# Graph network block on one core: packed key one-hots, made by six per-partition compares a window

## The chip, the cores and the metric

The kernel runs on one core of a Trainium2 chip. The metric is the device time of one execution in microseconds (us). TensorE, VectorE, ScalarE, GpSimd and SyncE run their own instruction streams and meet at semaphores.

## The reference

1250 nodes with 768 features and 40000 edges (src, dst), sorted by dst. A layer norm with relu, then a two-layer graph attention network (4 heads of 512, then one of 768), added to x; again a layer norm with relu, then two graph convolutions, added to x. Cut to what matters here:

```
h = relu(layernorm(x))
x = x + gat(elu(gat(h, 4 heads)), 1 head)     # softmax over the edges of each dst
h = relu(layernorm(x))
x = x + gcn(relu(gcn(h)))                     # sums over edges, scaled by degrees
gat: h = x @ W ; e = leaky_relu(al_s[src] + al_d[dst]) ; out[dst] = sum softmax(e) * h[src]
```

## The kernel before

Sparse sums are made dense. A matrix `counts` [src, dst], in ten src tiles of 128 rows, holds how many edges go from src to dst. Later stages use it as a factor of the weights. It is made on TensorE in the stage `first_layer`, beside the first product h = x @ W1.

**Edges.** The 40000 edges lie in 320 chunks of 125 (one edge a partition). The dst range is cut into 80 windows (`NW`) of 16 nodes. Because the edges are sorted, a window needs few chunks: `FIX` = 6 fixed ones each, and what is left goes through `extra_chunks`, a loop with one round here. An edge has a low part (src & 127, 0 to 127) and a key (dst in the window x 10 + src >> 7, 0 to 159, `WK` = 160). For each chunk the one-hot of the low parts (125 x 128) times the one-hot of the keys (125 x 160) adds the edge to its cell.

**One-hots (VectorE).** `count_hot(wd)` (L803) makes both one-hots of all six chunks of a window in one compare (L807): `codes` [125, 2, 160, 6] against `parts_of[:, wd]` [125, 2, 6], spread over the 160 values. The two halves are told apart by an offset of 16384 in codes and parts of the key half. The result goes to one of `SLOTS` = 7 slots of `hot` and lies as [half, value, chunk]: the values of one chunk are 6 bf16 elements, 12 bytes, apart.

**Counts (TensorE).** `count(wd)` (L1141) waits for `hot_ready` and runs six matmuls (L1147), one a chunk, with stationary operand hot[..., 0, 0:128, i] and moving operand hot[..., 1, :, i], both with the step of 12 bytes. The last one frees the slot (`hot_used`). ScalarE copies a group of three windows from PSUM to counts (`count_out`, L694).

**Order around the change.** It is written out by hand. TensorE runs 30 h tiles (`FIRST`; three heads of ten), each 18 f32 matmuls of 512 columns (`tile(n)`, L1134). After each of tiles 0 to 26 come the counts of `windows_after(n)`, 2 or 3 windows; after tile 28 `count_extra` (L1155). VectorE runs, for each n, the one-hots of the same windows, then `columns(n)` (four `attention_column`s, L858, for n = 0 to 2, 10 to 12, 20 to 22 and 26 to 28), `extra_chunks` (L814 to L849) at n = 28, and `weight_lo` (L801) at n = 9, 19 and 29. ScalarE copies each h tile to `stage` (L704), rounds the next head's weights (`weight_hi`, L689), and copies groups of counts. SyncE spills each stage slot (two slots) to memory (L640) and loads the next head's W1 at n = 6, 16 and 22, the last one behind a wait for the columns of head 2. Before this stage, `front` prepares the edges: GpSimd makes `codes` (L289), and VectorE makes parts_of (L421, L422).

Of the kernel before, what the change touches and what calls it, by code (L numbers as in the profile page):

```python
# [5 lines left out]
fp32 = mybir.dt.float32  # L6
f32r = mybir.dt.float32r
bf16 = mybir.dt.bfloat16
u16 = mybir.dt.uint16
i32 = mybir.dt.int32  # L10
ALU = mybir.AluOpType
# [3 lines left out]
P = 128  # L15
# [14 lines left out]
EC = 125  # L30
# [5 lines left out]
NW = NP // WD  # L36
WK = WD * T
FIX = 6
SLOTS = 7
OFFSET = 16384  # L40
# [43 lines left out]
class Memory:  # L84

    def __init__(self, nc, keep):
        base = (nc.sbuf_base + 31) // 32 * 32
# [29 lines left out]
        self.codes = edges("codes", [EC, 2, WK, FIX], u16)  # L117
        self.parts_of = edges("parts_of", [EC, NW, 2, FIX], u16)
# [10 lines left out]
        self.hot = heads("hot", [EC, SLOTS, 2, WK, FIX], bf16)  # L129
# [72 lines left out]
def front(nc, st, mem, x, src, dst, load_weights, tile_in):  # L202
# [3 lines left out]
    codes, parts_of, place, low, key = mem.codes, mem.parts_of, mem.place, mem.low, mem.key  # L206
# [52 lines left out]
    with nc.Block() as block:  # L259
# [9 lines left out]
        def _(pool_):  # L269
# [9 lines left out]
            nc.gpsimd.iota(base[:, :, :], pattern=[[-WK, NW], [0, FIX]], base=OFFSET, channel_multiplier=0).then_inc(made, 1)  # L279
# [9 lines left out]
            nc.gpsimd.iota(codes[:, :, :, :], pattern=[[OFFSET, 2], [1, WK], [0, FIX]], base=0, channel_multiplier=0).then_inc(made, 1)  # L289
# [61 lines left out]
        def _(dve):  # L351
# [61 lines left out]
            def window_parts():  # L413
                n = NW * FIX
                dve.wait_ge(picked, 1)
                chain(nc.vector.tensor_copy(s_i[:, :], p_e[:, 0, 0:n]), False)
                chain(nc.vector.scalar_tensor_tensor(out=d_f[:, :], in0=p_e[:, 1, 0:n], scalar=float(T),
                                                     in1=base_f[:, :, :].rearrange("e w i -> e (w i)"), op0=ALU.mult, op1=ALU.add))
                chain(nc.vector.tensor_scalar(s_hi[:, :], s_i[:, :], 7, None, ALU.logical_shift_right), False)
                chain(nc.vector.tensor_scalar(s_lo[:, :], s_i[:, :], P - 1, None, ALU.bitwise_and))  # L420
                chain(nc.vector.tensor_copy(parts_of[:, :, 0, :], s_lo[:, :].rearrange("e (w i) -> e w i", i=FIX)), False)  # L421
                chain(nc.vector.tensor_tensor(parts_of[:, :, 1, :], d_f[:, :].rearrange("e (w i) -> e w i", i=FIX),  # L422
                                              s_hi[:, :].rearrange("e (w i) -> e w i", i=FIX), ALU.add))
# [100 lines left out]
def first_layer(nc, st, mem, W2, b1, as2, ad2, h_scratch, w_in, a_in, load_weights, tile_in):  # L524
# [3 lines left out]
    xT, codes, parts_of, place, low, key = mem.xT, mem.codes, mem.parts_of, mem.place, mem.low, mem.key  # L528
# [85 lines left out]
    def count_bank(g):  # L614
        return banks[:, 2 + g % 2, :]
# [13 lines left out]
    with nc.Block() as block:  # L629
# [162 lines left out]
        def _(dve):  # L792
# [11 lines left out]
            def count_hot(wd):  # L804
                if wd >= SLOTS:
                    dve.wait_ge(hot_used, wd - SLOTS + 1)
                nc.vector.tensor_tensor(hot[:, wd % SLOTS, :, :, :], codes[:, :, :, :],  # L807
                                        parts_of[:, wd, :, :].unsqueeze(2).to_broadcast([EC, 2, WK, FIX]),
                                        ALU.is_equal).then_inc(hot_ready, 1)
# [308 lines left out]
        def _(pe):  # L1118
# [22 lines left out]
            def count(wd):  # L1141
                g, at = wd // WG, wd % WG * WK
                if at == 0 and g >= 2:
                    pe.wait_ge(win_out, g - 1)
                pe.wait_ge(hot_ready, wd + 1)
                for i in range(FIX):
                    last = nc.tensor.matmul(count_bank(g)[:, at:at + WK], hot[:, wd % SLOTS, 0, 0:P, i], hot[:, wd % SLOTS, 1, :, i],  # L1147
                                            start=i == 0, stop=i == FIX - 1)
                last.then_inc(hot_used, 1)
# [832 lines left out]
```

## Time and profile before

| | |
|---|---|
| median of 3 runs | 1326.92 us (1325.04 to 1327.08) |
| the profiled execution | 1326.07 us |
| its span, first to last instruction | 1324.2 us |
| TensorE (PE) busy | 1227.1 us |
| TensorE weight loads (PEld) | 1107.6 us |
| VectorE (DVE) busy | 850.8 us |
| ScalarE (ACT) busy | 510.6 us |
| mean granted TensorE clock | 0.952 of 2.4 GHz |

The profile is of one execution. Busy time is the union of the instructions' spans on an engine. Matmuls overlap in their rows: the duration of one is longer than the distance from its start to the next start, and it is that distance that TensorE's time is made of. The same holds, less so, for VectorE. In a timeline a row with xN merges N equal instructions, and its second number is the time from the first's start to the last's end.

### The profile page before, as it was taken

To read this page: it belongs to the slowest core of one execution; us is meant where nothing else is said; L and a number is where in the kernel's file an instruction comes from. 1 tells how busy PE (TensorE), PEld (TensorE's weight loads), DVE (VectorE), ACT (ScalarE), POOL (GpSimd) and SP (SyncE) were. 2 spreads that over 40 slices of the span, in tenths; PEclk is the share of its full clock that TensorE was granted. 3 is DMA by queue.
4 is the path that set the end of the run, shared out by engine and by line. 5 is a ranking of instruction groups with operands and counts; after the bars stand their busy time and mean duration, and the time that the engine had idled before them with its cause. 6 is when DMAs were issued, how large, how long until landed. Compare 5 with 4: busy or idle time off the path is not lost. (4 is left out here: it accounts for less than half of the span.)

```text
span 1324.2 us, 17459 instructions
## 1 busy us (share of the span) xinstructions
PE 1227.1 (93%) x7119; PEld 1107.6 (84%) x7119; DVE 850.8 (64%) x1372; ACT 510.6 (39%) x1037; POOL 25.5 (2%) x39
## 2 busy tenths in 40 slices
PE   2799999999989999999999999995899999999998
PEld 2576676776779999999999999994799999989998
DVE  7952733647579768876887678857886652351253
ACT  1311212112165555555555565512544552152111
POOL 5000000000010000000000000000000000000000
PEclk9788888889999999999999999997899999999999
DMA  5003021300011020102010201000310220010131
GB/s 189 14 27 96 31 57 64 91 29 25 0 56 49 1 80 1 49 1 80 1 48 1 80 1 49 1 0 13 117 48 25 92 73 1 1 36 0 65 113 58
DMA packets 27618, 58.44 MB, mean 44 GB/s; under 512 B 3492, under 2 KB 6152, under 8 KB 27536
## 3 DMA queue, kind: packets, MB, share of 16 engines
q1 hardware_dynamic: 27344, 56.96, 13.1%
q8 instruction: 59, 0.97, 0.3%
q10 hardware_dynamic: 192, 0.32, 0.1%
q14 instruction: 23, 0.19, 0.0%
HBM read 41.73 MB, written 15.54 MB: 43 GB/s over the span
## 5 line engine op out<-in xcount | busy, mean ns | idle before, releaser
L1250 PE MATMUL banks<-hs,ring_hi 128*128 128x258 f32 (+1 forms) x1600 | 300.7, 289 | 4.0 <-DVE ring_lo L507 2.1
L1250 PEld LDWEIGHTS banks<-hs,ring_hi 128*128 128x128 f32 (+1 forms) x1600 | 249.0, 189 | 5.7 <-issue 2.5
L1250 PE MATMUL banks<-hs,ring_lo 128*128 128x258 f32 (+1 forms) x800 | 227.4, 284 | 0.0
L481 ACT ACTIVATE e<-banks,al 128x256 f32<-128x256 f32 (+1 forms) x500 | 194.0, 491 | 22.4 <-PE banks L466 22.4
L1250 PEld LDWEIGHTS banks<-hs,ring_lo 128*128 128x128 f32 (+1 forms) x800 | 151.4, 189 | 0.0
L489 ACT ACTIVATE ring_hi<-pf 128x512 fp32r<-128x512 f32 (+1 forms) x125 | 81.7, 654 | 158.6 <-DVE pf L500 155.4
L807 DVE TENSOR_TENSOR hot<-codes,parts_of 125x1920 bf16<-125x1920 uint16 x80 | 90.2, 1155 | 78.9 <-PE banks L1147 78.6
L1278 PE MATMUL banks<-w_hi,oT_hi 128*128 128x384 f32 (+1 forms) x320 | 110.3, 345 | 11.3 <-DVE rows L997 5.5
L1134 PE MATMUL banks<-w_hi,xT_hi 128*128 128x512 f32 x240 | 111.7, 466 | 3.5 <-DVE w_lo L801 3.5
L1147 PE MATMUL banks<-hot 125*128 125x160 bf16 x480 | 110.2, 401 | 0.0
L498 DVE TENSOR_TENSOR e<-e 128x512 f32<-128x512 f32 (+1 forms) x125 | 84.5, 676 | 39.1 <-ACT e L481 39.0
L1278 PE MATMUL banks<-w_lo,oT_hi 128*128 128x384 f32 (+1 forms) x320 | 109.5, 342 | 0.0
L1278 PE MATMUL banks<-w_hi,oT_lo 128*128 128x384 f32 (+1 forms) x320 | 109.5, 342 | 0.0
L1134 PE MATMUL banks<-w_hi,xT_lo 128*128 128x512 f32 x240 | 104.8, 436 | 0.0
L1134 PE MATMUL banks<-w_lo,xT_hi 128*128 128x512 f32 x240 | 104.4, 435 | 0.0
L1147 PEld LDWEIGHTS banks<-hot 125*128 125x128 bf16 x480 | 58.6, 128 | 45.8 <-issue 7.1
L704 ACT ACTIVATE stage<-banks 128x512 f32<-128x512 f32 x30 | 17.9, 595 | 183.3 <-PE banks L1134 183.3
L500 DVE SCALAR_TENSOR_TENSOR pf<-e,counts 128x512 f32<-128x512 f32 (+1 forms) x125 | 85.0, 680 | 4.3
L507 DVE TENSOR_TENSOR ring_lo<-pf,ring_hi 128x512 fp32r<-128x512 f32 (+1 forms) x125 | 84.1, 673 | 2.3 <-ACT ring_hi L489 1.7
L1829 PE MATMUL banks<-hs_hi,ring_hi 128*128 128x386 f32 x200 | 70.4, 352 | 7.8 <-DVE ring_lo L507 6.3
L997 DVE TENSOR_TENSOR rows<-rows,banks 128x384 f32<-128x384 f32 (+1 forms) x80 | 43.9, 551 | 45.5 <-PE banks L1278 44.3
L1278 PEld LDWEIGHTS banks<-w_hi,oT_hi 128*128 128x128 f32 (+1 forms) x320 | 60.3, 189 | 13.7 <-DVE rows L997 6.8
(267 smaller groups left out, 2250.3 us busy)
## 6 DMA issues: line engine op xcount, KB each, us to landing
h_scratch<-stage SPq DMA_DIRECT2D x30, 256.0 KB, 2.0
hs<-h_scratch SPq DMA_DIRECT2D x30, 256.0 KB, 2.9
w_st<-in_L_gnn_W SPq DMA_DIRECT2D x4, 1536.0 KB, 10.2
w_st<-in_L_gnn_W SPq DMA_DIRECT2D x16, 384.0 KB, 3.5
gw_st<-in_L_gnn_W SPq DMA_DIRECT2D x12, 384.0 KB, 3.8
xr<-in_x SPq DMA_DIRECT2D x9, 384.0 KB, 6.8
rows<-in_x SPq DMA_DIRECT2D x9, 384.0 KB, 3.4
x_scratch<-rows SPq DMA_DIRECT2D x9, 384.0 KB
```

Source lines behind the costliest of these rows:

```text
L481: last = nc.scalar.activation(self.e[:, local % 2, a, i, 0:n], self.p_shift[:, a, 0:n], ACT.Exp, bias=scores[a][:, g * G + i:g * G + i + 1])
L489: nc.scalar.activation(self.ring[0][:, g, :, 0:n], self.pf[:, (c * NG + g) % 2, :, 0:n], ACT.Copy)\
L498: nc.vector.tensor_tensor(e[:, 0], e[:, 0], e[:, 1], ALU.max).then_inc(self.e_max, 1)
L500: nc.vector.scalar_tensor_tensor(out=self.pf[:, local % 2, :, 0:n], in0=e[:, 0], scalar=1.0, in1=counts[:, g * G:(g + 1) * G, d0:d0 + n], ...
L507: nc.vector.tensor_tensor(self.ring[1][:, g, :, 0:n], self.pf[:, (c * NG + g) % 2, :, 0:n], self.ring[0][:, g, :, 0:n].bitcast(fp32), ALU. ...
L807: nc.vector.tensor_tensor(hot[:, wd % SLOTS, :, :, :], codes[:, :, :, :], parts_of[:, wd, :, :].unsqueeze(2).to_broadcast([EC, 2, WK, FIX] ...
L997: nc.vector.tensor_tensor(acc, acc, p_g[i % 2][0:m, 0:HALF], ALU.add).then_inc(g_out, 1)
L1134: last = nc.tensor.matmul(p_h[n % 2], xT[a][:, k, t * P:(t + 1) * P], w[b][:, k, :], start=u == 0, stop=u == 3 * KD - 1)
L1147: last = nc.tensor.matmul(count_bank(g)[:, at:at + WK], hot[:, wd % SLOTS, 0, 0:P, i], hot[:, wd % SLOTS, 1, :, i], start=i == 0, stop=i = ...
L1250: last = nc.tensor.matmul(p_a[0:m, dt, half, 0:HH], wt.ring[a][:, s // G, s % G, dt * P:dt * P + m], hs[:, s, b, half * HH:(half + 1) * HH ...
L1278: last = nc.tensor.matmul(p_g[i % 2][0:m, 0:HALF], oT[a][:, k, dt * P:dt * P + m], w2[b][:, k, half * HALF:(half + 1) * HALF], start=j == ...
L1829: last = nc.tensor.matmul(p_a(t)[0:m, half, 0:AH], wt.ring[a][:, s // G, s % G, dt * P:dt * P + m], hs[b][:, s, half * AH:(half + 1) * AH] ...
```

## The change

- `hot` becomes one flat row a slot: first the low one-hots as [value, chunk] (768 elements, step 12 bytes as before), then for each chunk its key one-hot as a packed row of 160.
- `count_hot` makes the low half with one compare of two tensors (768 elements), and each of the six key one-hots with a compare of `place` (0, 1, 2, ... in 16 bits) against a per-partition fp32 key, `keys_of[:, wd, i]`. The slot's semaphore is raised by the last of them.
- The matmuls take the same stationary values at the same step, and a packed moving operand.
- codes has the low half alone; parts_of has the low parts, in 16 bits; keys_of is new, in fp32; the offset of 16384 is gone.

```diff
-        self.codes = edges("codes", [EC, 2, WK, FIX], u16)
-        self.parts_of = edges("parts_of", [EC, NW, 2, FIX], u16)
+        self.codes = edges("codes", [EC, P, FIX], u16)
+        self.parts_of = edges("parts_of", [EC, NW, FIX], u16)
+        self.keys_of = edges("keys_of", [EC, NW, FIX], fp32)
...
-        self.hot = heads("hot", [EC, SLOTS, 2, WK, FIX], bf16)
+        self.hot = heads("hot", [EC, SLOTS, FIX * (P + WK)], bf16)
...
-            nc.gpsimd.iota(base[:, :, :], pattern=[[-WK, NW], [0, FIX]], base=OFFSET, channel_multiplier=0).then_inc(made, 1)
+            nc.gpsimd.iota(base[:, :, :], pattern=[[-WK, NW], [0, FIX]], base=0, channel_multiplier=0).then_inc(made, 1)
...
-            nc.gpsimd.iota(codes[:, :, :, :], pattern=[[OFFSET, 2], [1, WK], [0, FIX]], base=0, channel_multiplier=0).then_inc(made, 1)
+            nc.gpsimd.iota(codes[:, :, :], pattern=[[1, P], [0, FIX]], base=0, channel_multiplier=0).then_inc(made, 1)
...
-                chain(nc.vector.tensor_copy(parts_of[:, :, 0, :], s_lo[:, :].rearrange("e (w i) -> e w i", i=FIX)), False)
-                chain(nc.vector.tensor_tensor(parts_of[:, :, 1, :], d_f[:, :].rearrange("e (w i) -> e w i", i=FIX),
+                chain(nc.vector.tensor_copy(parts_of[:, :, :], s_lo[:, :].rearrange("e (w i) -> e w i", i=FIX)), False)
+                chain(nc.vector.tensor_tensor(keys_of[:, :, :], d_f[:, :].rearrange("e (w i) -> e w i", i=FIX),
                                               s_hi[:, :].rearrange("e (w i) -> e w i", i=FIX), ALU.add))
...
-                nc.vector.tensor_tensor(hot[:, wd % SLOTS, :, :, :], codes[:, :, :, :],
-                                        parts_of[:, wd, :, :].unsqueeze(2).to_broadcast([EC, 2, WK, FIX]),
-                                        ALU.is_equal).then_inc(hot_ready, 1)
+                part = hot[:, wd % SLOTS, :]
+                nc.vector.tensor_tensor(part[:, 0:FIX * P].rearrange("e (v i) -> e v i", i=FIX), codes[:, :, :],
+                                        parts_of[:, wd, :].unsqueeze(1).to_broadcast([EC, P, FIX]), ALU.is_equal)
+                for i in range(FIX):
+                    last = nc.vector.tensor_scalar(part[:, FIX * P + i * WK:FIX * P + (i + 1) * WK], place[0:EC, 0:WK],
+                                                   keys_of[:, wd, i:i + 1], None, ALU.is_equal)
+                last.then_inc(hot_ready, 1)
...
+                part = hot[:, wd % SLOTS, :]
+                lows = part[:, 0:FIX * P].rearrange("e (v i) -> e i v", i=FIX)
                 for i in range(FIX):
-                    last = nc.tensor.matmul(count_bank(g)[:, at:at + WK], hot[:, wd % SLOTS, 0, 0:P, i], hot[:, wd % SLOTS, 1, :, i],
+                    last = nc.tensor.matmul(count_bank(g)[:, at:at + WK], lows[:, i, :], part[:, FIX * P + i * WK:FIX * P + (i + 1) * WK],
```

On TensorE, ScalarE and SyncE the order of instructions is the same. On VectorE each compare becomes seven instructions. The place is VectorE's queue from the columns of tile 0 on, through tile 1's windows to the first column of tile 1 (L858 before, L863 now, is an attention column with the read of its sum). Before:

```order
L858 ISA vcol 128x1
L807 TENSOR_TENSOR hot<-codes,parts_of 125x1920 x3
L858 ISA junk,vcol<-w_st,abc 128x512 [waits v_done]
L858 ISA vcol 128x1
L858 ISA junk,vcol<-w_st,abc 128x512 [waits v_done]
```

Now:

```order
L863 ISA vcol 128x1
L809 TENSOR_TENSOR hot<-codes,parts_of 125x768
L812 TENSOR_SCALAR hot<-place,keys_of 125x160 x6
L809 TENSOR_TENSOR hot<-codes,parts_of 125x768
L812 TENSOR_SCALAR hot<-place,keys_of 125x160 x6
L809 TENSOR_TENSOR hot<-codes,parts_of 125x768
L812 TENSOR_SCALAR hot<-place,keys_of 125x160 x6
L863 ISA junk,vcol<-w_st,abc 128x512 [waits v_done]
```

Three instructions have become 21, in the same place between the columns. From the third window of tile 2 on, the first instruction of a window waits for a free slot. Before:

```order
L807 TENSOR_TENSOR hot<-codes,parts_of 125x1920 x2
L807 TENSOR_TENSOR hot<-codes,parts_of 125x1920 [waits hot_used]
L858 ISA junk,vcol<-w_st,abc 128x512 [waits v_done]
L858 ISA vcol 128x1
```

Now:

```order
L809 TENSOR_TENSOR hot<-codes,parts_of 125x768
L812 TENSOR_SCALAR hot<-place,keys_of 125x160 x6
L809 TENSOR_TENSOR hot<-codes,parts_of 125x768 [waits hot_used]
L812 TENSOR_SCALAR hot<-place,keys_of 125x160 x6
L863 ISA junk,vcol<-w_st,abc 128x512 [waits v_done]
```

The wait stands at the window's first instruction in both.

## Rows read from the trace of the kernel before

**Rows 1.** The page's part 1: engine, busy us (share), instructions.
```profile
PE 1227.1 (93%) x7119; PEld 1107.6 (84%) x7119; DVE 850.8 (64%) x1372; ACT 510.6 (39%) x1037; POOL 25.5 (2%) x39
```

**Rows 2.** The page's part 5: group, count | busy us, mean ns | idle before, releaser.
```profile
L807 DVE TENSOR_TENSOR hot<-codes,parts_of 125x1920 bf16<-125x1920 uint16 x80 | 90.2, 1155 | 78.9 <-PE banks L1147 78.6
...
L1147 PE MATMUL banks<-hot 125*128 125x160 bf16 x480 | 110.2, 401 | 0.0
```

**Rows 3.** Timeline around one count stretch: start us, us, engine, line, operation, count.
```profile
150.09 0.39 PE L1134 MATMUL banks<-w_hi,xT_lo 128*128 128x512 f32 x1
...
153.50 0.39 PE L1134 MATMUL banks<-w_hi,xT_lo 128*128 128x512 f32 x1
...
153.72 4.13 PE L1147 MATMUL banks<-hot 125*128 125x160 bf16 x18
...
157.51 0.77 PE L1134 MATMUL banks<-w_hi,xT_hi 128*128 128x512 f32 x1
...
158.51 0.63 PE L1134 MATMUL banks<-w_hi,xT_lo 128*128 128x512 f32 x1
...
158.94 0.63 PE L1134 MATMUL banks<-w_hi,xT_hi 128*128 128x512 f32 x1
```

**Rows 4.** Windows: stretch, length, busy of PE, PEld, DVE, ACT, POOL, granted clock, DMA.
```profile
57.30:294.00 236.70, 236.70 (x950) 164.99 (x949) 124.05 (x184) 38.31 (x65) 0.00 (x0) 0.88 0.18 57
```

**Rows 5.** By source line, the count matmuls, then the extra chunk's: ns min/median/max.
```profile
L1147 PEld LDWEIGHTS banks<-hot x480: 124/127/145, 57.3 to 293.7; 125*128 125x128 bf16 x160
L1147 PE MATMUL banks<-hot x480: 392/402/403, 57.4 to 293.9; 125*128 125x160 bf16 x160
...
L1155 PEld LDWEIGHTS banks<-extra x1: 96/96/96, 303.8 to 303.8; 125*128 125x128 bf16 x1
L1155 PE MATMUL banks<-extra x1: 243/243/243, 303.8 to 303.8; 125*128 125x160 bf16 x1
```

**Rows 6.** Timeline of TensorE in the attention sums.
```profile
702.80 0.28 PE L1250 MATMUL banks<-hs,ring_lo 128*128 128x258 f32 x1
...
702.93 0.19 PEld L1250 LDWEIGHTS banks<-hs,ring_hi 128*128 128x128 f32 x1
...
703.16 0.28 PE L1250 MATMUL banks<-hs,ring_lo 128*128 128x258 f32 x1
```

**Rows 7.** Timeline of VectorE: one-hot compares, attention columns, the extra chunk's compares.
```profile
70.29 7.57 DVE L807 TENSOR_TENSOR hot<-codes,parts_of 125x1920 bf16<-125x1920 uint16 x7
...
151.97 0.68 DVE L858 CUSTOM_DVE_ANT_0 junk<-w_st,abc 128x512 bf16<-128x512 f32 x1
...
152.58 0.68 DVE L858 CUSTOM_DVE_ANT_0 junk<-w_st,abc 128x512 bf16<-128x512 f32 x1
...
299.69 0.27 DVE L844 TENSOR_SCALAR extra<-place,own_low 125x160 bf16<-125x160 uint16 x1
...
299.87 0.26 DVE L845 TENSOR_SCALAR extra<-place,own_key 125x160 bf16<-125x160 uint16 x1
```

**Rows 8.** Timeline of 20 small matmuls, and windows of the stretches around and behind them.
```profile
324.43 2.39 PE L1178 MATMUL banks<-ident,al_row 8*128 8x8 f32 x20
...
324.40:328.00 3.60, 3.60 (x26) 3.35 (x26) 3.50 (x7) 1.87 (x2) 0.00 (x0) 1.00 0.02 5
328.00:331.50 3.50, 3.50 (x10) 2.70 (x9) 3.43 (x3) 0.00 (x0) 0.00 (x0) 0.51 0.00 0
```

**Rows 9.** Timeline of VectorE, the first instruction of extra_chunks.
```profile
295.75 0.06 DVE L814 MEMSET round__493<- 128x1 f32 x1 [11.96 <-ACT counts L694]
```

**Rows 10.** The page's part 6: DMA issues, KB each, median us to landing.
```profile
h_scratch<-stage SPq DMA_DIRECT2D x30, 256.0 KB, 2.0
...
w_st<-in_L_gnn_W SPq DMA_DIRECT2D x4, 1536.0 KB, 10.2
```

**Rows 11.** Timeline of GpSimd in front.
```profile
3.84 2.81 POOL L289 IOTA codes<- 125x1920 uint16 x1
...
20.27 11.78 POOL L293 TENSOR_SCALAR xr<-xr,rstd,nmr 128x768 f32<-128x768 f32 x10 [13.26 <-DVE nmr L431]
```

More of the change, by code:

```diff
@@ L205, in front @@
     ident, ones, pick, xT = mem.ident, mem.ones, mem.pick, mem.xT
-    codes, parts_of, place, low, key = mem.codes, mem.parts_of, mem.place, mem.low, mem.key
+    codes, parts_of, keys_of, place, low, key = mem.codes, mem.parts_of, mem.keys_of, mem.place, mem.low, mem.key
     until, reach, total = mem.until, mem.reach, mem.total
@@ L527, in first_layer @@
     mask, rows, vcol, deg = mem.mask, mem.rows, mem.vcol, mem.deg
-    xT, codes, parts_of, place, low, key = mem.xT, mem.codes, mem.parts_of, mem.place, mem.low, mem.key
+    xT, codes, parts_of, keys_of, place, low, key = mem.xT, mem.codes, mem.parts_of, mem.keys_of, mem.place, mem.low, mem.key
     until, reach, total = mem.until, mem.reach, mem.total
```

## The prediction

> **What bounds the kernel now.** I read the engine table first. TensorE is busy for 93% of the span and VectorE for 64% [rows 1], so what counts is time on TensorE. The groups by cost then show the two instructions that the change touches [rows 2]. The 480 count matmuls are busy for 110.2 us, and the 80 one-hot compares on VectorE sat idle 78.9 us before they ran, nearly all of it for TensorE. So VectorE is ahead of TensorE in this stage and waits for a free slot of the seven. The place is the stretch from 57 to 294 us, in which h tiles 0 to 26 alternate with the counts of two or three windows each.
>
> The timeline of one tile gives the prices [rows 3]. The f32 matmuls of 512 columns start 0.227 us apart ((153.50 - 150.09) / 15), so a tile of 18 takes 4.09 us. The 18 count matmuls take 157.51 - 153.72 = 3.79 us, 0.2105 us each, though each streams only 160 columns. Right behind them the f32 matmuls start 0.43 us apart (158.51 to 158.94): that is the lower clock, 1.2 GHz. Over the whole stretch the granted clock is 0.88 [rows 4], so 0.12 x 236.7 = 28 us are lost to it. The stretch adds up: 26 x 4.09 + 480 x 0.2105 + 28 = 235 us against 236.7.
>
> **TensorE's part of the change.** The moving operand (key one-hots) goes from a step of 12 bytes to a packed row; the stationary one (low one-hots) keeps its 12-byte step. The kernel holds one packed count matmul of the same shape, the extra chunk's: 243 ns against 402 ns, and its weight load 96 ns against 127 ns [rows 5]. The 159 ns are 160 columns at about 1 ns more each, which fits a moving read that is too slow when strided. A packed operand leaves 160 / 2.4 GHz = 67 ns of streaming. The 512-column matmul takes 227 ns for 213 ns of streaming, 14 ns over, and I add that: 0.081 us each. The weight loads stay strided. The f32 matmuls of 258 columns start (703.16 - 702.80) / 3 = 0.12 us apart beside weight loads of 0.19 us [rows 6], so a load longer than the spacing is covered by the matmul in front; a strided load of 0.127 us should be too. Gain: 480 x (0.2105 - 0.081) = 62 us. Bounds: 0.067 (no gap at all) to 0.127 (loads of 127 ns not overlapped among themselves).
>
> The clock: it falls after 3.79 us in which the array streamed 67 of every 210 ns. Afterwards that stretch is 18 x 0.081 = 1.46 us, 67 of 81 ns streaming. The nearest row is the 20 matmuls of 8 columns, 2.39 us with almost nothing streamed: the clock stood at full through 328 us and then fell to 0.51 for 3.5 us [rows 8]. The new stretch is shorter and dense, so I expect the full clock back, 28 us. The Trainium skill (TensorE: Matmul & The Clock Gate, Part 1) says that the default is throttled and that activity releases it; by it too a denser stretch is kept at 2.4 GHz, and the fall in rows 3 behind sparse counts agrees.
>
> **VectorE's part.** Today one compare of 1920 elements takes (7.57 - 1.16) / 6 = 1.07 us a window. The new one has 768 elements: by proportion 0.43 us, and 0.47 with a fixed share that doesn't shrink. The six key compares have an exact counterpart in the extra chunk's code, a 125x160 compare with an fp32 per-partition key: the two start 0.18 us apart, each lasting 0.26 to 0.27 [rows 7]. Six at 0.18 are 1.08 us. A window costs 0.47 + 1.08 = 1.55 us, 0.48 more than now, 38 us more in 80 windows. Bounds of one key compare: 0.09 (its share of the 1920-element row) to 0.265 (no overlap with the next). The Trainium skill (VectorE: DVE Perf Modes, the errata section) gives 58 cycles and a quarter of the elements for such an operation, 102 ns; by that figure a window would cost VectorE no more than now, and no wait below would arise. The row at 0.18 decides.
>
> Does that cover hold? A tile now costs TensorE 4.09 + 1.46 = 5.55 us, VectorE 3 x 1.55 = 4.65 us. That is still covered. But in tiles 0 to 2, 10 to 12 and 20 to 22 VectorE also makes four attention columns of 0.61 us [rows 7], 2.45 us together: 7.1 us. Neither the first tiles nor those behind a weight_lo (which ties VectorE to TensorE at tiles 9 and 19) have slots in hand, so TensorE waits some 1.55 us in each of nine tiles (shifted by one, tiles 1 to 3, 11 to 13, 21 to 23): 14 us. In these the counts are spread out and the clock may fall as now. Most of such a slow phase lies inside the next wait; for the last tile of each run I keep 1.5 us, 4 us in all. Everything else behind that semaphore moves with it.
>
> The end of the stage: VectorE sat idle 11.96 us before extra_chunks [rows 9], waiting for the last counts. Its work from there (12 columns, 7.3 us, and the chunk, 4.4 us) now starts with the last counts, against two tiles, 8.2 us, on TensorE. With VectorE some 3 us ahead by tile 26 this costs 0.5 us; with no lead 3.5.
>
> Weight and scratch DMAs: W1's load lands 10.2 us after issue, a spill of h 2.0 us [rows 10], and SyncE issues both in order. At tile 22 the load also waits for columns(22), which are now late: it lands some 16 us after that tile, and the spill behind it at about 18.5. ScalarE's copy of tile 24 waits for that spill; TensorE needs that copy for tile 26, at about 21 us. Covered, with 2 us to spare. On GpSimd codes gets shorter (2.81 us now), but the engine idles 13.26 us behind it [rows 11]: nothing. The 32-bit keys_of is written once by the instruction that wrote half of parts_of: nothing I can price.
>
> **Sum.** Against the profiled execution of 1326.07 us (span 1324.2 and 1.9 around it, 0.85 below the median of the three runs): -62 (counts) - 28 (clock) + 14 (waits) + 4 (clock in those tiles) + 0.5 (end) = -71.5, so **1254.5 us**. Of a measurement of this kernel about 0.2% can be told from no change.
>
> **Rivals.**
> - *The clock still falls after every count stretch.* For it: in rows 8 a stretch shorter than today's was followed by a fall. Against: that one streamed nearly nothing. TensorE then takes 28 us more, but the slow tiles hide most of the 14 us of waiting: about 1268 us. Chance 0.12.
> - *The strided weight loads set the spacing.* They were hidden behind 210 ns and would now show. At 0.127 us the counts cost 22 us more, the waits shrink by half: 1269 us, with the clock falling too up to 1286. Chance 0.12.
> - *The stride was not the price.* If the 0.21 us came from the weights' stride, which stays, nothing moves on TensorE, VectorE's longer windows fit in a tile of 9.1 us (7.1), and the time stays at 1326. The Trainium skill (SBUF — State Buffer, the note on cachelines) lets one stride up to 8 bf16 for free, and by that a step of 6 elements costs nothing. The packed row of 243 ns speaks against it, as the only difference there is packing, but its weights are packed too. Chance 0.06.
> - *VectorE becomes the bound throughout.* At 0.265 us a key compare a window costs 2.06 us, a tile 6.2 against 5.55. The stage is then 26 x 6.2 + 22 (columns) + 8 (weight_lo) = 191 us instead of 165: 1281 us. Chance 0.07.
> - *VectorE makes it slower.* The same mechanism beyond its turning point: 80 windows and the 30 us of columns and weight_lo exceed 236.7 us from 2.58 us a window, that is 0.35 us a key compare, twice the row. At 0.40 the stage takes 260 us: 1349 us. Only a loss of the packed rate that rows 7 don't show would do it. Chance 0.03.
>
> **How the numbers follow.** The forecast has the remaining 0.60; its own range is 1240 (compares at 0.09, no waits) to 1265. The range goes down to 1238 for a spacing near 0.067 with few waits, and up to 1286, which takes in the lower clock, weight loads and VectorE as bound; outside are the two cases near 1326 and above, and some tail. Faster 0.91, within 0.2% 0.06, slower 0.03.
>
> **What will show it.** Count matmuls with starts about 0.08 us apart; MATMUL rows of about 243 ns with weight loads still at 127; a granted clock above 0.95 in the stage; key compares 0.18 us apart, 480 of them; VectorE's idle time before the one-hots far below 78.9 us and TensorE waiting for hot, in tiles 1 to 3, 11 to 13 and 21 to 23 alone; the last counts near 222 us instead of 294. It is wrong if the spacing stays above 0.13, if the clock stays at 0.88, or if TensorE waits for VectorE in every tile.

## The result and the profile after

The changed kernel takes 1241.26 us (median of 4 runs, 1237.08 to 1245.65), the kernel before 1326.69 us (1325.04 to 1327.08). The ratio is 0.9359 (95% interval 0.9324 to 0.9393). The forecast was 1254.5 us, range 1238 to 1286; the measured time lies near the lower end. The profiled execution took 1237.08 us, with a span of 1235.0.

The page of the changed kernel, parts 1 and 5. The line of L812 answers to the compare of [rows 2]; the page has no count matmuls any more among its costliest groups.

```profile
PE 1126.2 (91%) x7119; PEld 1052.8 (85%) x7119; DVE 881.1 (71%) x1852; ACT 508.2 (41%) x1037; POOL 23.9 (2%) x39
...
L812 DVE TENSOR_SCALAR hot<-place,keys_of 125x160 bf16<-125x160 uint16 x480 | 89.2, 260 | 0.0
```

TensorE's busy time fell by 101 us, VectorE's rose by 30. VectorE no longer stands idle ahead of its compares: 78.9 us in [rows 2], nothing now, before L809 or L812.

The count matmuls by source line, in the columns of [rows 5], and from the view of the waits how long TensorE's matmuls sat idle for hot (us, times, the longest):

```profile
L1154 PEld LDWEIGHTS banks<-hot x480: 124/125/148, 57.5 to 212.4; 125*128 125x128 bf16 x160
L1154 PE MATMUL banks<-hot x480: 232/233/274, 57.6 to 212.5; 125*128 125x160 bf16 x160
...
PE banks L1154 <- DVE hot L812: 9.1, 15, 0.9
```

The matmul row is 233 ns instead of 402; the weight load, whose step did not change, is as it was. The last counts start at 212.5 us instead of 293.9.

The timeline shows an undisturbed count stretch, with the f32 matmul behind it, and then what VectorE's columns do to a later one:

```profile
115.69 1.45 PE L1154 MATMUL banks<-hot 125*128 125x160 bf16 x18
116.93 0.48 PE L1139 MATMUL banks<-w_hi,xT_hi 128*128 128x512 f32 x1
...
125.57 0.56 DVE L809 TENSOR_TENSOR hot<-codes,parts_of 125x768 bf16<-125x768 uint16 x1
126.04 1.11 DVE L812 TENSOR_SCALAR hot<-place,keys_of 125x160 bf16<-125x160 uint16 x6
127.07 0.55 DVE L809 TENSOR_TENSOR hot<-codes,parts_of 125x768 bf16<-125x768 uint16 x1
...
127.88 0.62 PE L1154 MATMUL banks<-hot 125*128 125x160 bf16 x6
128.79 0.59 PE L1154 MATMUL banks<-hot 125*128 125x160 bf16 x6 [0.29 <-DVE hot L812]
...
130.20 0.62 PE L1154 MATMUL banks<-hot 125*128 125x160 bf16 x6 [0.81 <-DVE hot L812]
```

In the first row 18 matmuls start (1.45 - 0.233) / 17 = 0.072 us apart, against (4.13 - 0.402) / 17 = 0.219 before. Counted as the prediction counted its 0.2105, up to the start of the f32 matmul behind them, it is (116.93 - 115.69) / 18 = 0.069. A window costs VectorE 127.07 - 125.57 = 1.50 us (six compares at 0.172 and one at 0.47). In the tile with columns the second and third windows are late by 0.29 and 0.81 us. Such waits of about 0.3 us occur in six tiles, those of about 0.8 us in nine. Idle time is less than what a wait costs, because the rows of undisturbed matmuls overlap: the twelve matmuls from 127.88 to 130.20 take 2.32 us where 12 x 0.072 = 0.86 would do, 1.46 us more for 1.10 us of idle time. Summed in this way over the trace, the waits cost 12.2 us.

The windows, in the columns of [rows 4]: the stage from first to last count, then to the end of the h tiles, then the rest. Each is the changed kernel's, and then the kernel before's:

```profile
57.55:212.90 155.35, 145.94 (x951) 119.45 (x951) 150.47 (x644) 35.60 (x66) 0.00 (x0) 1.00 0.27 85
212.90:286.90 74.00, 71.25 (x345) 54.07 (x343) 50.65 (x89) 18.45 (x33) 0.23 (x3) 1.00 0.04 15
286.90:1235.00 948.10, 885.69 (x5723) 859.02 (x5722) 632.53 (x1015) 441.39 (x921) 7.54 (x6) 0.98 0.12 40
```

```profile
57.35:294.30 236.95, 236.95 (x950) 165.29 (x950) 124.00 (x184) 38.31 (x65) 0.00 (x0) 0.88 0.18 57
294.30:371.30 77.00, 74.24 (x345) 56.26 (x344) 47.04 (x77) 18.53 (x33) 0.23 (x3) 0.96 0.03 11
371.30:1324.20 952.90, 892.66 (x5723) 865.98 (x5722) 632.45 (x1015) 441.01 (x921) 7.53 (x6) 0.97 0.12 40
```

The stage went from 236.95 to 155.35 us, 81.6 less, and its clock from 0.88 to 1.00. The next stretch gave 3.0 us, with the clock at 1.00 instead of 0.96, and all the rest 4.8, at 0.98 instead of 0.97. No instruction of those two stretches changed. Another profiled execution of the same changed kernel (1248.17 us) has the same three stretches at these places:

```profile
59.00:213.90 154.90, 145.85 (x950) 119.37 (x950) 149.96 (x643) 35.50 (x66) 0.00 (x0) 1.00 0.27 86
213.90:291.30 77.40, 74.64 (x345) 56.48 (x344) 50.73 (x91) 18.52 (x33) 0.23 (x3) 0.96 0.04 14
291.30:1246.20 954.90, 895.05 (x5723) 868.73 (x5722) 632.39 (x1015) 440.93 (x921) 7.54 (x6) 0.97 0.12 40
```

Its stage is as short, 154.9 us, but behind it nothing is gained: 77.4 and 954.9 us, against 77.0 and 952.9 before. So the stage's own gain is some 82 us and repeats; what the first profile gained behind it goes with the clock there and does not. The changed kernel's scatter between executions comes from behind the stage.

### The profile page after: what moved, and what is told of

Its sections match the earlier page's. It is cut to its first block and busy times, and to the rows that moved or that the text cites. A ratio compares the mean times of both kernels' runs of the same rounds, so it can differ in the third digit from the quotient of the medians.

```text
span 1235.0 us, 17939 instructions
## 1 busy us (share of the span) xinstructions
PE 1126.2 (91%) x7119; PEld 1052.8 (85%) x7119; DVE 881.1 (71%) x1852; ACT 508.2 (41%) x1037; POOL 23.9 (2%) x39
## 5 line engine op out<-in xcount | busy, mean ns | idle before, releaser
L1257 PE MATMUL banks<-hs,ring_hi 128*128 128x258 f32 (+1 forms) x1600 | 297.7, 287 | 4.9 <-DVE z L974 2.8
L1257 PEld LDWEIGHTS banks<-hs,ring_hi 128*128 128x128 f32 (+1 forms) x1600 | 246.5, 187 | 6.7 <-DVE z L974 3.0
L490 ACT ACTIVATE ring_hi<-pf 128x512 fp32r<-128x512 f32 (+1 forms) x125 | 81.6, 653 | 157.7 <-DVE pf L501 154.6
L1285 PE MATMUL banks<-w_hi,oT_hi 128*128 128x384 f32 (+1 forms) x320 | 109.6, 342 | 12.7 <-DVE rows L1002 6.9
L1139 PE MATMUL banks<-w_hi,xT_hi 128*128 128x512 f32 x240 | 97.4, 406 | 3.5 <-DVE w_lo L802 3.5
L1139 PE MATMUL banks<-w_lo,xT_hi 128*128 128x512 f32 x240 | 94.4, 393 | 0.0
L1139 PE MATMUL banks<-w_hi,xT_lo 128*128 128x512 f32 x240 | 94.2, 393 | 0.0
L812 DVE TENSOR_SCALAR hot<-place,keys_of 125x160 bf16<-125x160 uint16 x480 | 89.2, 260 | 0.0
L1836 PE MATMUL banks<-hs_lo,ring_hi 128*128 128x386 f32 x200 | 68.5, 342 | 0.0
L1836 PE MATMUL banks<-hs_hi,ring_lo 128*128 128x386 f32 x200 | 68.2, 341 | 0.0
```

The lines of the kernel that those rows point to most:

```text
L490: nc.scalar.activation(self.ring[0][:, g, :, 0:n], self.pf[:, (c * NG + g) % 2, :, 0:n], ACT.Copy)\
L812: last = nc.vector.tensor_scalar(part[:, FIX * P + i * WK:FIX * P + (i + 1) * WK], place[0:EC, 0:WK], keys_of[:, wd, i:i + 1], None, ALU.i ...
L1139: last = nc.tensor.matmul(p_h[n % 2], xT[a][:, k, t * P:(t + 1) * P], w[b][:, k, :], start=u == 0, stop=u == 3 * KD - 1)
L1257: last = nc.tensor.matmul(p_a[0:m, dt, half, 0:HH], wt.ring[a][:, s // G, s % G, dt * P:dt * P + m], hs[:, s, b, half * HH:(half + 1) * HH ...
L1285: last = nc.tensor.matmul(p_g[i % 2][0:m, 0:HALF], oT[a][:, k, dt * P:dt * P + m], w2[b][:, k, half * HALF:(half + 1) * HALF], start=j == ...
L1836: last = nc.tensor.matmul(p_a(t)[0:m, half, 0:AH], wt.ring[a][:, s // G, s % G, dt * P:dt * P + m], hs[b][:, s, half * AH:(half + 1) * AH] ...
```

## The experiments

Theory A is the prediction's: the moving operand's step was the price and pulled the clock down with it; VectorE's price is the spacing of its compares, and what is left of its cost is a wait where attention columns share a tile with three windows. Unless said otherwise, an edit stands against the changed kernel. Where a stage is given in us, it runs from the first to the last count.

### A long count stretch that is dense

```diff
+                for again in range(3):
-                for i in range(FIX):
+                    for i in range(FIX):
```

> Each window's six count matmuls run three times over (each round starts the sums anew, so the counts are the same). A count stretch is then 54 matmuls at 0.072 us, 3.9 us, as long as the 3.79 us stretch of the kernel before, but dense. Theory A (sparse streaming, not the length of the stretch or its small matmuls, lets the clock fall): granted clock 1.00 from the first to the last count; stage 26 x 4.09 + 1440 x 0.072 = 210 us, no wait for VectorE; time 1241 + 210 - 155 = 1296 us. Rival (a stretch of 3.8 us of these matmuls costs the clock in any case): clock 0.88 to 0.90 in the stage, 1320 us or more.

Measured: 1300.89 us (1300.72 to 1302.54). The timeline and the windows:

```profile
168.41 3.94 PE L1155 MATMUL banks<-hot 125*128 125x160 bf16 x54
...
60.00:200.00 140.00, 140.00 (x1258) 123.44 (x1255) 102.72 (x447) 23.59 (x40) 0.00 (x0) 1.00 0.20 65
```

54 matmuls take as long as the 18 did before, (3.94 - 0.233) / 53 = 0.070 us apart, and the clock stays at 1.00. It was not the length of the stretch that brought it down. The stage is 209 us (210 expected); the time is 5 us above what I expected, and that lies behind the stage.

### The roles exchanged

```diff
-                nc.vector.tensor_tensor(part[:, 0:FIX * P].rearrange("e (v i) -> e v i", i=FIX), codes[:, :, :],
-                                        parts_of[:, wd, :].unsqueeze(1).to_broadcast([EC, P, FIX]), ALU.is_equal)
+                nc.vector.tensor_tensor(part[:, FIX * P:].rearrange("e (v i) -> e v i", i=FIX), codes[:, :, :],
+                                        parts_of[:, wd, :].unsqueeze(1).to_broadcast([EC, WK, FIX]), ALU.is_equal)
                 for i in range(FIX):
-                    last = nc.vector.tensor_scalar(part[:, FIX * P + i * WK:FIX * P + (i + 1) * WK], place[0:EC, 0:WK],
-                                                   keys_of[:, wd, i:i + 1], None, ALU.is_equal)
+                    last = nc.vector.tensor_scalar(part[:, i * P:(i + 1) * P], place[0:EC, 0:P],
+                                                   lows_of[:, wd, i:i + 1], None, ALU.is_equal)
...
+                keys = part[:, FIX * P:].rearrange("e (v i) -> e i v", i=FIX)
-                    last = nc.tensor.matmul(count_bank(g)[:, at:at + WK], lows[:, i, :], part[:, FIX * P + i * WK:FIX * P + (i + 1) * WK],
+                    last = nc.tensor.matmul(count_bank(g)[:, at:at + WK], part[:, i * P:(i + 1) * P], keys[:, i, :],
```

> Roles exchanged: the stationary low one-hots are packed (six compares of 128 with a per-partition value), the moving key one-hots keep the step of 12 bytes (one two-tensor compare of 960). Theory A (the moving operand's step is the price): matmul starts 0.21 to 0.22 us apart, weight loads 96 ns, clock falls again to 0.88, VectorE hidden, time 1320 to 1330 us as the kernel before. Rival (the stationary operand's step was the price and the change helped in another way): starts 0.07 to 0.08 us apart, time 1235 to 1250 us.

Measured: 1319.76 us (1315.04 to 1323.87), ratio to the kernel before 0.9949 (0.9925 to 0.9973).

```profile
107.42 4.00 PE L1154 MATMUL banks<-hot 125*128 125x160 bf16 x18
...
L1154 PEld LDWEIGHTS banks<-hot x480: 96/116/126, 58.2 to 287.2; 125*128 125x128 bf16 x160
L1154 PE MATMUL banks<-hot x480: 372/392/394, 58.2 to 287.4; 125*128 125x160 bf16 x160
...
60.00:200.00 140.00, 140.00 (x583) 95.61 (x581) 100.86 (x425) 22.37 (x38) 0.00 (x0) 0.90 0.19 62
```

The starts are (4.00 - 0.392) / 17 = 0.212 us apart. Nearly the whole loss of the kernel before is back, clock included (0.90), although this kernel too makes seven compares a window and has a packed stationary operand. The moving operand's step is the cause. The stage takes 229.7 us, 7.3 less than before. Summed over the distances between starts, 3.4 us of it are in the count matmuls (7 ns each, 0.212 against 0.219) and 3.9 in the f32 matmuls, whose clock is 0.90 and not 0.88. These together are about the 5.5 us by which this kernel beats the one before (1325.28 us in the same set of runs).

### Everything packed

```diff
-                nc.vector.tensor_tensor(part[:, 0:FIX * P].rearrange("e (v i) -> e v i", i=FIX), codes[:, :, :],
-                                        parts_of[:, wd, :].unsqueeze(1).to_broadcast([EC, P, FIX]), ALU.is_equal)
+                for i in range(FIX):
+                    nc.vector.tensor_scalar(part[:, i * P:(i + 1) * P], place[0:EC, 0:P],
+                                            parts_of[:, wd, i:i + 1], None, ALU.is_equal)
```

> The low one-hots are packed as well, by six more compares of 128 elements in place of the two-tensor one. Theory A (strided weight loads are hidden behind the matmul in front, and compares cost 0.17 us each): weight loads 96 instead of 125 ns, matmul starts unchanged at 0.072 us, a window costs VectorE 12 x 0.17 = 2.04 us, stage 80 x 2.04 + 30 = 193 us, time about 1279 us. Rival (the strided weight loads still cost TensorE time): starts closer than 0.070 us, and the time below 1279 by what 480 of them give.

Measured: 1277.16 us (1273.24 to 1278.65).

```profile
107.57 1.00 PE L1154 MATMUL banks<-hot 125*128 125x160 bf16 x12
...
109.00 0.59 PE L1154 MATMUL banks<-hot 125*128 125x160 bf16 x6 [0.42 <-DVE hot L813]
...
L1154 PEld LDWEIGHTS banks<-hot x480: 95/98/152, 59.1 to 245.4; 125*128 125x128 bf16 x160
```

The load rows shrink from 125 to 98 ns, and twelve starts are (1.00 - 0.233) / 11 = 0.070 us apart instead of 0.072. The median distance of all of them is 0.069 us in both kernels, so beside a packed moving operand the strided weight load is hidden. Twelve compares cost VectorE 2.0 us a window, and TensorE now waits also in tiles without columns (109.00). In the tiles with columns it waits 1.3 to 1.5 us at a time, and the clock from 60 to 200 us is 0.94. The stage takes 186.5 us (193 expected). The change left the right half strided: packing it too costs 36 us.

### The key compares made twice

```diff
+                for i in range(FIX):
+                    last = nc.vector.tensor_scalar(mem.spare[:, wd % SLOTS, i * WK:(i + 1) * WK], place[0:EC, 0:WK],
+                                                   keys_of[:, wd, i:i + 1], None, ALU.is_equal)
                 last.then_inc(hot_ready, 1)
```

> The six key compares are made a second time into a spare tile, so a window costs VectorE 1.49 + 6 x 0.172 = 2.52 us; TensorE's instructions are unchanged. Theory A (VectorE's price is the spacing of 0.172 us, and near 2.58 us a window it eats the whole gain): stage 80 x 2.52 + 22 + 8 = 232 us, TensorE waits for hot in every tile, time about 1317 us. Rival (compares overlap with something or VectorE's work is largely hidden): below 1290 us.

Measured: 1320.23 us (1316.23 to 1328.06), ratio to the kernel before 0.9957 (0.9932 to 0.9983).

```profile
105.68 0.56 DVE L810 TENSOR_TENSOR hot<-codes,parts_of 125x768 bf16<-125x768 uint16 x1
107.17 1.12 DVE L816 TENSOR_SCALAR spare<-place,keys_of 125x160 bf16<-125x160 uint16 x6
108.20 0.56 DVE L810 TENSOR_TENSOR hot<-codes,parts_of 125x768 bf16<-125x768 uint16 x1
...
113.40 0.62 PE L1158 MATMUL banks<-hot 125*128 125x160 bf16 x6 [1.84 <-DVE spare L816]
...
60.00:200.00 140.00, 105.55 (x576) 83.26 (x576) 140.00 (x683) 20.94 (x38) 0.00 (x0) 0.89 0.20 60
```

A window costs 108.20 - 105.68 = 2.52 us and the stage 228 us (232 expected). At this price of VectorE nearly the whole gain is gone, close to the turning point of 2.58 us that the prediction gave for its last rival. The row of windows adds one thing: with TensorE idle for a quarter of the time, 1.84 us at a stretch, the clock is down to 0.89. VectorE is busy for all 140.00 us of that row, so it is VectorE that sets this stage's length and not TensorE's clock.

### One key compare of two tensors

```diff
-                for i in range(FIX):
-                    last = nc.vector.tensor_scalar(part[:, FIX * P + i * WK:FIX * P + (i + 1) * WK], place[0:EC, 0:WK],
-                                                   keys_of[:, wd, i:i + 1], None, ALU.is_equal)
+                last = nc.vector.tensor_tensor(part[:, FIX * P:].rearrange("e (i v) -> e i v", i=FIX),
+                                               mem.key_codes[:, :].unsqueeze(1).to_broadcast([EC, FIX, WK]),
+                                               keys_of[:, wd, :].unsqueeze(2).to_broadcast([EC, FIX, WK]), ALU.is_equal)
```

> The six key compares become one two-tensor compare of 960 elements that writes the same packed rows; its key operand repeats each value 160 times (step 0 in the innermost direction), in 16 bits. Theory A (the repeated operand takes the packed rate away, one element a cycle): about 1.05 us for the 960 elements, the same as six compares at 0.172, waits for hot near 9 us and the time 1241 us as the changed kernel. Rival (it keeps two elements a cycle): 0.58 us, a window costs 1.05 us as before the change, TensorE waits for hot no more, time about 1232 us.

Measured: 1245.58 us (1243.32 to 1250.0).

```profile
103.19 1.14 DVE L813 TENSOR_TENSOR hot<-key_codes,keys_of 125x960 bf16<-125x960 uint16 x1
104.26 0.55 DVE L811 TENSOR_TENSOR hot<-codes,parts_of 125x768 bf16<-125x768 uint16 x1
```

The compare takes 104.26 - 103.19 = 1.07 us, 960 elements at 1.1 ns, and the waits for hot are 10.5 us. Six compares of 0.172 and this one cost nearly the same. The old compare took 1.07 us for 1920 elements [rows 7]; its operands had adjacent elements innermost. The repeated innermost value halves the rate.

### The columns spread over more tiles

```diff
-                    for k in (2 * t, 2 * t + 1):
-                        for a in range(2):
-                            attention_column(i, k, a)
+                many = 2 if i < 2 else 4
+                for m in range(2 * KD)[many * t:many * (t + 1)]:
+                    attention_column(i, m // 2, m % 2)
```

> The attention columns of heads 0 and 1 are made two a tile over six tiles in place of four a tile over three; head 2 is left. Theory A (TensorE waits because columns and one-hots of a tile, 3 x 1.49 + 2.45 = 6.9 us, exceed its 5.4 us): a tile with two columns needs 5.7 us, so in tiles 1 to 6 and 11 to 16 the waits for hot shrink to about 0.3 us each, in tiles 21 to 23 they stay at 1.1; in all 9.1 falls to about 6 us, and the time to about 1238. Rival (the waits come from too few slots or from the semaphore's way): they stay at 9 us.

Measured: 1232.82 us (1232.2 to 1241.54, 6 runs), ratio 0.9332 (0.9304 to 0.9359).

```profile
PE banks L1153 <- DVE hot L812: 3.0, 5, 0.8
```

The waits fell from 9.1 to 3.0 us (6 expected), and the stage from 155.2 to 149.1. The waits do come from the columns, as theory A says; they fell by more than expected. The stage's 6.1 us are shown. The time is not told from the changed kernel's: the two ratios, 0.9332 and 0.9359, have intervals that overlap, and the six runs span 9 us.

### Two key compares on GpSimd

```diff
-                for i in range(FIX):
+                for i in range(FIX - BY_POOL):
...
+            for wd in range(NW):
+                if wd >= SLOTS:
+                    pool_.wait_ge(hot_used, wd - SLOTS + 1)
+                part = hot[:, wd % SLOTS, :]
+                for i in range(FIX - BY_POOL, FIX):
+                    last = nc.gpsimd.tensor_scalar(part[:, FIX * P + i * WK:FIX * P + (i + 1) * WK], place[0:EC, 0:WK],
+                                                   keys_of[:, wd, i:i + 1], None, ALU.is_equal)
+                last.then_inc(pool_ready, 1)
```

> GpSimd, idle in this stage, makes the key one-hots of two of the six chunks; VectorE makes four (1.15 us a window, 3.4 us a tile, 5.9 with columns, against TensorE's 5.4). Theory A (VectorE's surplus in the column tiles is the whole of what is left, and the two engines do not hinder each other): waits for hot fall from 9.1 to about 2 us, time about 1234 us, provided that GpSimd needs under 0.9 us a compare. Rival (GpSimd is slower than that, or they slow each other): TensorE waits for GpSimd in every tile, time above 1245 us.

Measured: 1237.72 us (1235.35 to 1241.93), ratio 0.9342 (0.9324 to 0.9361).

```profile
L678 POOL TENSOR_SCALAR hot<-place,keys_of x160: 674/798/1722, 50.9 to 203.1; 125x160 bf16<-125x160 uint16 x160
...
141.14 0.54 DVE L819 TENSOR_TENSOR hot<-codes,parts_of 125x768 bf16<-125x768 uint16 x1
142.29 0.55 DVE L819 TENSOR_TENSOR hot<-codes,parts_of 125x768 bf16<-125x768 uint16 x1
142.52 4.97 POOL L678 TENSOR_SCALAR hot<-place,keys_of 125x160 bf16<-125x160 uint16 x6 [1.58 <-PE banks L1165]
...
144.96 0.54 DVE L819 TENSOR_TENSOR hot<-codes,parts_of 125x768 bf16<-125x768 uint16 x1
145.43 1.05 DVE L822 TENSOR_SCALAR hot<-place,keys_of 125x160 bf16<-125x160 uint16 x4
146.40 0.55 DVE L819 TENSOR_TENSOR hot<-codes,parts_of 125x768 bf16<-125x768 uint16 x1
```

This lies between the two expectations. GpSimd is fast enough (0.80 us), but where it works all the time VectorE's windows start up to 1.44 us apart (146.40 - 144.96), and up to 1.55 in tiles with columns, not the 1.15 that I expected: four compares take as long as six did. Where GpSimd stands idle (the 1.58 us before 142.52) a window does cost 142.29 - 141.14 = 1.15 us. So GpSimd's work slows VectorE's; which resource they share was not isolated, and why GpSimd's own compares range from 0.67 to 1.7 us stays open. Waits for hot are still 6.5 us, and a gain over the changed kernel (0.9359 +- 0.0034) is not shown.

### The step of either operand

```diff
+PROBES = [(1, 1), (1, 2), (1, 3), (1, 4), (1, 5), (1, 6), (1, 8), (1, 10), (0, 1), (0, 3), (0, 4), (0, 8), (0, 12)]
...
+                kind, step = PROBES[wd % len(PROBES)]
+                for i in range(FIX):
+                    still = part[:, i * P:(i + 1) * P] if kind else part[:, 0:P * step].rearrange("e (v s) -> e s v", s=step)[:, 0, :]
+                    moving = part[:, 0:WK * step].rearrange("e (v s) -> e s v", s=step)[:, 0, :] if kind else part[:, FIX * P + i * WK:FIX * P + (i + 1) * WK]
+                    nc.tensor.matmul(count_bank(g)[:, at:at + WK], still, moving, start=i == 0, stop=i == FIX - 1)
```

> Ahead of each window's six matmuls stand six probe matmuls into the same bank (the real ones start the sums anew, so the counts are right). By window in turn they read a moving operand of 160 columns at a step of 1, 2, 3, 4, 5, 6, 8 and 10 elements of 2 bytes beside a packed stationary one, and then a stationary operand of 128 columns at a step of 1, 3, 4, 8 and 12 beside a packed moving one. Theory A (a moving read is slowed from the step at which fewer than two elements fall into 16 bytes): starts 0.07 us apart up to step 4, then rising, 0.21 at 6, and no more than some 0.25 at 8 and 10; with the stationary steps 0.07 us throughout, only their load rows grow. Rival (a step of up to 8 elements is free and something else slowed the old layout): 0.07 us at step 6 and 8. Rival (price in proportion to the bytes skipped): 0.11 at step 2, 0.14 at 4, 0.35 at 10.

Measured: 1293.96 us in one execution; what counts here is its timeline. Four windows with moving steps of 2, 3, 6 and 8 elements; L1158 are six probes, L1160 the six real ones behind them:

```profile
97.10 0.61 PE L1158 MATMUL banks<-hot 125*128 125x160 bf16 x6
97.55 0.58 PE L1160 MATMUL banks<-hot 125*128 125x160 bf16 x6
97.96 0.81 PE L1158 MATMUL banks<-hot 125*128 125x160 bf16 x6
98.61 0.58 PE L1160 MATMUL banks<-hot 125*128 125x160 bf16 x6
...
105.95 1.45 PE L1158 MATMUL banks<-hot 125*128 125x160 bf16 x6
107.22 0.60 PE L1160 MATMUL banks<-hot 125*128 125x160 bf16 x6
107.66 1.87 PE L1158 MATMUL banks<-hot 125*128 125x160 bf16 x6
109.34 0.60 PE L1160 MATMUL banks<-hot 125*128 125x160 bf16 x6
```

The distance from a probe row to the real row behind it, over six, is what one matmul of 160 columns costs:

| step of the moving operand, elements of 2 bytes | 1 | 2 | 3 | 4 | 5 | 6 | 8 | 10 |
|---|---|---|---|---|---|---|---|---|
| us a matmul | 0.070 | 0.075 | 0.108 | 0.142 | 0.177 | 0.212 | 0.280 | 0.285 |

The table takes one window of each kind. The medians over all six or seven windows of a kind lie within 0.001 us of it, but for step 2 with 0.072. With a stationary step of 1, 3, 4, 8 or 12 beside a packed moving operand the median is 0.069 us throughout. None of the three expectations holds as a whole. Theory A had steps 5 and 6 about right, 3 and 4 wrong (there is no threshold at four), and 8 and 10 too low by 0.03 us. The second, that steps up to 8 elements are free, and with it the rule that the prediction quotes in its third rival, is wrong for this operand. The third is right at step 4 and wrong at 2 and 10. What the rows show is a price in proportion to the step from 3 to 8, 0.035 us an element (0.28 / 8), hidden up to step 2 behind the 67 ns that 160 columns take at 2.4 GHz, and no higher at 10 than at 8.

One reading fits all eight numbers: a fetch of 16 bytes for every 1.75 ns (0.28 us / 160). At step 3 the 160 columns span 60 such pieces, 0.105 us, at step 6 120, 0.21 us, and from step 8 on every column needs one of its own. It is a reading and not shown by itself.

### A version that uses this: keys in pairs

Two chunks' key one-hots are interleaved. The moving step is 2 elements, and every operand of the compare has two adjacent elements.

```diff
+                last = nc.vector.tensor_tensor(part[:, FIX * P:].rearrange("e (h v j) -> e h v j", v=WK, j=2),
+                                               mem.key_codes[:, :, :].unsqueeze(1).to_broadcast([EC, FIX // 2, WK, 2]),
+                                               keys_of[:, wd, :].rearrange("e (h j) -> e h j", j=2).unsqueeze(2)
+                                               .to_broadcast([EC, FIX // 2, WK, 2]), ALU.is_equal)
...
+                keys = part[:, FIX * P:].rearrange("e (h v j) -> e h j v", v=WK, j=2)
-                    last = nc.tensor.matmul(count_bank(g)[:, at:at + WK], lows[:, i, :], part[:, FIX * P + i * WK:FIX * P + (i + 1) * WK],
+                    last = nc.tensor.matmul(count_bank(g)[:, at:at + WK], lows[:, i, :], keys[:, i // 2, i % 2, :],
```

> The key one-hots of two chunks are interleaved (three pairs, the values of a chunk 4 bytes apart), so that one two-tensor compare of 960 elements makes all six with adjacent elements on every side. Theory A (the moving read is free up to a step of 4 bytes, as the probes gave 0.075 us, and the compare keeps two elements a cycle when its operands' last direction has step 1): matmul starts 0.075 us apart, the compare 0.58 us, a window costs VectorE 1.05 us as before the change, a column tile 5.6 us against TensorE's 5.45, waits for hot under 2 us in place of 9, time 1232 to 1236 us. Rival (the run of two elements is too short for the packed rate): the compare takes 1.05 us, waits stay near 9 us, time 1243 us.

> Key pairs as above, and the attention columns of heads 0 and 1 spread over six tiles. Theory A: no waits for hot but in the first tiles, time as the kernel with pairs alone or up to 1 us less (1231 to 1235 us), since nothing of VectorE is left on TensorE's path in this stage. Rival (column spreading has a gain of its own, as its run at 1232.8 us might suggest): some 5 us less than with pairs alone.

> The changed kernel as it is, beside the two above on one chip, so that they can be compared: 1241 us, runs spread over 1237 to 1246 by where the clock falls in later stages; waits for hot 9 us; stage from the first to the last count 155 us.

Measured on one chip, against the same runs of the kernel before (1325.17 us):

| | us (lowest to highest) | ratio (95%) |
|---|---|---|
| changed kernel again | 1241.77 (1237.52 to 1248.17) | 0.9363 (0.9342 to 0.9384) |
| keys in pairs | 1231.92 (1228.55 to 1235.15) | 0.9300 (0.9278 to 0.9323) |
| pairs, and columns spread | 1231.52 (1230.87 to 1233.28) | 0.9299 (0.9282 to 0.9316) |

The kernel with pairs, its count stretch, VectorE's compares and its groups:

```profile
67.89 1.52 PE L1158 MATMUL banks<-hot 125*128 125x160 bf16 x18
70.09 0.56 DVE L811 TENSOR_TENSOR hot<-codes,parts_of 125x768 bf16<-125x768 uint16 x1
70.56 0.65 DVE L813 TENSOR_TENSOR hot<-key_codes,keys_of 125x960 bf16<-125x960 uint16 x1
71.13 0.55 DVE L811 TENSOR_TENSOR hot<-codes,parts_of 125x768 bf16<-125x768 uint16 x1
...
L811 DVE TENSOR_TENSOR hot<-codes,parts_of 125x768 bf16<-125x768 uint16 x80 | 44.1, 551 | 12.7 <-PE banks L1158 12.7
```

The starts are (1.52 - 0.234) / 17 = 0.076 us apart, the key compare takes 0.57 us and a window 71.13 - 70.09 = 1.04. TensorE's matmuls wait for hot nowhere, and VectorE waits for TensorE again (12.7 us). This is 10 us below the change in the same set of runs; it is not told from the run with the columns spread alone (0.9332, 0.9304 to 0.9359). Spreading the columns adds nothing to it: the stage is 144.4 us long in both. That fits with spreading having helped only by those waits.

## Why the prediction was right, point by point

- **The matmul spacing** was forecast at 0.081 us and measured at 0.069 in the same count, 0.072 from start to start. The direction and the cause hold. Summed over the stage, the count matmuls outside of waits went from 100.8 to 33.7 us, 67 us less where the term said 62. What was off is the 14 ns that I added from the f32 matmuls of 512 columns: for these bf16 ones of 160 it is 2 to 5 ns. A fixed gap does not carry over from one matmul to another.
- **The weight loads are hidden.** Held: 0.069 us at the median with packed and with strided loads.
- **The clock** came back in full. The f32 matmuls' distances in the stage fell from 129.7 to 103.1 us, 26.6 us where the forecast had 28. The 4 us that I took off for tiles with waits were not needed: waits of 0.3 and 0.8 us left the clock at 1.00. Waits of 1.3 to 1.5 us in the column tiles (everything packed, 0.94) and of up to 1.84 us in most tiles (compares twice, 0.89) did not.
- **A window on VectorE** was forecast at 1.55 us and measured at 1.50; the compare at 0.172 instead of 0.18.
- **The waits.** Their place was right: tiles 1 to 3, 11 to 13, 21 to 23. The 9.1 us of idle time are not their price; in distances between starts, which is how the 14 us were worked out, they cost 12.2. A column tile costs VectorE 3 x 1.50 + 2.45 = 6.95 us, and two such tiles follow each other 6.93 us apart (123.27 to 130.20), 1.5 us more than a tile without (5.44). I set nine times that; six tiles paid it in full, and the first of each run less, since VectorE had some lead there.
- **The end of the stage** (0.5 us), the load at tile 22 and GpSimd: nothing showed. extra_chunks had no idle time before it, yet its matmul did not wait.
- **Sum.** The stage should have given 72 us and gave 81.6. The three terms explain it but for 0.3 us: 4.9 from the spacing, 2.6 from the clock (26.6 against 28 - 4) and 1.8 from the waits are 9.3, all three in the same direction. The other 3.6 us between 1254.5 and the median lie behind the stage. I had not given those stretches a term, and the two profiles show them anywhere from 7.8 us shorter to 2.4 us longer than before. So in the stage no error hid another one, and no run explains the 3.6 us behind it.

The rivals: the clock falling in any case and the weight loads as the bound are refuted; "the stride was not the price" is refuted by the exchanged roles; VectorE as the bound in every tile is what happens at 2.0 us a window, and nearly all of the gain is lost at 2.52.

## What to carry to other kernels

Read the distance between starts of small matmuls against columns / 2.4 GHz: where it is a multiple, look at the step of the moving operand first, since that of the stationary one was hidden here. The price was paid twice, 67 us in the matmuls and 27 in the clock of what follows them. A layout with two adjacent elements can serve both engines: nearly free for TensorE's read (0.072 against 0.069 us), and enough for VectorE's faster rate (0.57 instead of 1.07 us for 960 elements).

## What the runs showed that I had not expected

- The moving read costs in proportion to its step between 3 and 8 elements of 2 bytes, 0.035 us an element for 160 columns, and no more beyond: 0.280 us at 8, 0.285 at 10.
- A compare whose second operand repeats one value in the innermost direction runs at 1.1 ns an element (1.07 us for 960); with pairs of adjacent elements the same 960 take 0.57 us.
- GpSimd's compares stretch VectorE's: a window with four key compares took 1.36 to 1.55 us where GpSimd worked throughout, 1.15 where it stood idle, against 1.50 with six alone.
- A wait costs more than its idle time: 12.2 us for 9.1 in the changed kernel, since the matmuls beside it no longer overlap.
- Runs of the changed kernel scatter over 8 to 11 us. Two profiles of it differ by 11.2 us in span, all but 1.0 of it behind the stage (3.4 in the next stretch, 6.8 in the rest), where no instruction was touched. Why the clock falls there in some runs more than in others stays open. Runs of the kernel before scatter as widely where there are many of them: 1321.39 to 1332.55 us over 19.
